# ScalarE fetches the last piece of every eighth group row by row, beside SyncE's three in eight

## What is computed

```python
h = relu(layernorm(x))
# first layer: relational convolution, 8 edge types
xW  = einsum('nd,rde->nre', h, W_rel)
agg = segment_sum(xW[src, edge_type], dst)
g   = gelu(layernorm(agg + h @ W_self + b_conv)); y = h + g
x   = x + y + (gelu(layernorm(y) @ W1 + b1) @ W2 + b2)
# second layer: attention with 4 heads of 32
h   = relu(layernorm(x)); xt = h @ W.T + bias
alpha = leaky_relu(alpha_src[src] + alpha_dst[dst])
x   = x + segment_sum(xt[src] * segment_softmax(alpha, dst), dst)
```

## Time and profile before

| | |
|---|---|
| time, median of 3 runs | 4385.58 us (4385.05 to 4386.91) |
| profiled execution, its own time | 4389.14 us |
| its span, first to last instruction | 4387.2 us |
| GpSimd busy | 3111.7 us, 71% of the span |
| VectorE, TensorE, ScalarE busy | 2539.8, 2471.2, 851.8 us |
| transfers of one row issued by SyncE | 4736 in each stage |

### The profile page before, as it was taken

One profiled execution on the slowest core, in us unless ns is written; L12 is line 12 of the kernel. 1 busy time (PEld: TensorE's weight loads), 2 busy tenths in 40 slices (PEclk: granted clock), 3 DMA queues, 4 the chain that ended last, 5 costly groups with the idle time before them and its releaser, 6 DMA issues.

```text
span 4387.2 us, 66590 instructions
## 1 busy us (share of the span) xinstructions
PE 2471.2 (56%) x13797; PEld 2079.8 (47%) x13902; DVE 2539.8 (58%) x7085; ACT 851.8 (19%) x2937; POOL 3111.7 (71%) x3284
## 2 busy tenths in 40 slices
PE   8833444444444444444444666666666666666665
PEld 3332443344334333334334555556566555565555
DVE  7742343343434434344345777777777777777777
ACT  5400110111101111011112222222222222222222
POOL 2177777777777777777737777777777777777774
PEclk9966676777777777777676777777777777777877
DMA  9622222222222222222214222222222222222221
GB/s 319 255 54 54 59 64 60 61 62 59 64 59 62 62 59 64 59 62 62 58 38 114 56 59 61 59 59 61 59 62 59 59 62 59 62 59 59 61 58 45
DMA packets 187072, 314.55 MB, mean 72 GB/s; under 512 B 67132, under 2 KB 117910, under 8 KB 185977
## 3 DMA queue, kind: packets, MB, share of 16 engines
q0 software_dynamic: 104128, 216.79, 21.2%
q1 hardware_dynamic: 38907, 68.15, 4.5%
q10 hardware_dynamic: 43634, 25.41, 2.0%
HBM read 238.50 MB, written 71.59 MB: 71 GB/s over the span
## 4 chain that ended last, share of the span: by engine, by line
POOL 37%; issue 28%; PE 21%; DVE 9%; DMA 2%; ACT 2%; DVEq 0%; POOLq 0%; ACTq 0%; SPq 0%
POOL G L612 37%; PE bank L1696 9%; PE quad L1741 3%; PE quad L1747 2%; DMA xt_table<-w_all 2%; DVE A L1226 1%; PE quad L1736 1%; PE quad L1638 1%; PE bank L1638 1%; PE bank L1639 1%; PE quad L1639 1%; ACT w_all L822 1%; PE quad L1783 1%; DVE stats L183 1%; PE bank L1769 1%
## 5 line engine op out<-in xcount | busy, mean ns | idle before, releaser
L612 POOL DMA_INDIRECT G<-rel_table,idx x1611 | 1532.1, 951 | 637.5 <-issue 491.4
L612 POOL DMA_INDIRECT G<-xt_table,idx x1627 | 1539.8, 946 | 557.5 <-issue 557.5
L1828 PEld LDWEIGHTS quad<-ident,top 128*128 128x128 f32 x3328 | 581.6, 275 | 227.9 <-issue 227.4
L1828 PE MATMUL quad<-ident,top 128*128 128x128 f32 x3328 | 595.3, 362 | 146.7 <-DVEq L1430 146.7
L1191 DVE SCALAR_TENSOR_TENSOR agg<-bank,sel,agg 128x128 f32 x208 | 63.5, 346 | 995.9 <-PE bank L1696 980.4
L1859 PE MATMUL bank<-M,onehot 128*128 128x132 f32 x3328 | 438.4, 287 | 156.6 <-DVE M L1479 152.2
L1859 PEld LDWEIGHTS bank<-M,onehot 128*128 128x128 f32 x3328 | 404.2, 196 | 188.4 <-issue 188.4
L1696 PE MATMUL bank<-G,onehot 128*128 128x128 f32 x1638 | 270.4, 342 | 362.0 <-issue 349.4
L1696 PEld LDWEIGHTS bank<-G,onehot 128*128 128x128 f32 x1638 | 266.6, 259 | 366.5 <-issue 366.5
L1844 PE MATMUL bank<-Z,w_all 128*128 128x8 f32 x832 | 159.4, 320 | 373.4 <-issue 363.8
L881 ACT ACTIVATE M<-G,M 128x32 f32<-128x32 f32 x1664 | 363.8, 308 | 13.6 <-ACT M L876 0.4
(11 more groups left out here) (324 smaller groups left out, 3618.9 us busy)
## 6 DMA issues: line engine op xcount, KB each, us to landing
side<-rel_table SPq DMA_DIRECT2D x4736, 0.5 KB
side<-xt_table SPq DMA_DIRECT2D x4736, 0.5 KB
rel_table<-G SPq DMA_DIRECT2D x98, 512.0 KB, 3.5
G<-rel_table,idx POOLq DMA_INDIRECT x1627, 2.5
G<-xt_table,idx POOLq DMA_INDIRECT x1627, 7.0
xt_table<-w_all ACTq DMA_DIRECT2D x23, 264.0 KB
x_mid<-X ACTq DMA_DIRECT2D x23, 256.0 KB
out<-A ACTq DMA_DIRECT2D x23, 256.0 KB
```

The source lines that it names most:

```text
L612: g.indirect_dma_start(out=G[:, s, c, 0:width], out_offset=None, in_=table, in_offset=bass.IndirectOffsetOnAxis(ap=idx[:, s, c:c + 1], axi ...
L1828: ins = t.matmul(banks[j][:, hd * P:(hd + 1) * P], top[:, j, hd:hd + 1].to_broadcast([P, P]), ident[:, :], start=False, stop=(hd == HEADS ...
```

## The change

Eleven more groups leave their last piece out of GpSimd's gathers: 16, 24, 32, ... 96. ScalarE fetches these rows, with the same one-row transfers, into a fourth side buffer, and by a third line of places. GpSimd so issues 15 gathers for these groups too, in both stages.

In the first stage (`first_rows`) the line is loaded behind the index copy of the third group ahead of the target, and 32 rows with two register loads of 16 stand behind each of the index copies of the groups target - 2 to target + 1. In the attention (`att_rows`) the line is loaded in the round of group target - 11, and 16 rows with one register load stand behind the index copy in each of the eight rounds target - 10 to target - 3. ScalarE then copies the buffer into `G` as for the others. SyncE's rows stay as they are, and only the values of its waits are counted anew.

```diff
+ACT_STEP = 8
+ACT_FIRST, ACT_LAST = 16, 96
+ACT_ROWS = 16
...
+def by_sync(g):
+    return g <= ROW_LAST and g % ROW_OF in ROW_AT
+def by_act(g):
+    return ACT_FIRST <= g <= ACT_LAST and g % ACT_STEP == 0
 def by_rows(g):
-    return g <= ROW_LAST and g % ROW_OF in ROW_AT
-ROWED = [g for g in range(GROUPS) if by_rows(g)]
+    return by_sync(g) or by_act(g)
+ROWED = [g for g in range(GROUPS) if by_sync(g)]
+ACTED = [g for g in range(GROUPS) if by_act(g)]
+MOVED = [g for g in range(GROUPS) if by_rows(g)]
...
-        line = sb("line", [1, 2, P], i32)
-        side = sb("side", [P, SIDES, XT])
+        line = sb("line", [1, 3, P], i32)
+        side = sb("side", [P, SIDES + 1, XT])
...
+            def act_line_load(k, gr):
+                act.dma_start(line[0:1, 2, :], row_places[gr:gr + 1, k, :]).then_inc(act_line, 16)
+            def act_rows(k, gr, lo, hi):
+                q = ACTED.index(gr)
+                if lo == 0:
+                    act.wait_ge(act_line, 16 * (k * len(ACTED) + q + 1))
+                    if k == 0 and q:
+                        act.wait_ge(agg_done, ACTED[q - 1] + 1)
+                    elif k and q:
+                        act.wait_ge(side_moved, MOVED.index(ACTED[q - 1]) + 1)
+                    elif k:
+                        act.wait_ge(agg_done, ACTED[-1] + 1)
+                    act_stop(act)
+                for p in range(lo, hi, ACT_ROWS):
+                    places = load_places(mybir.EngineType.Activation, k, line[0:1, 2, p:p + ACT_ROWS], ACT_ROWS)
+                    for j in range(ACT_ROWS):
+                        act.dma_start(row_into(k, SIDES, p + j), row_at(k, places[j])).then_inc(acted[k], 16)
+            def first_rows(gr):
+                for target in ACTED:
+                    if gr == target - 3:
+                        act_line_load(0, target)
+                    if 0 <= gr - (target - 2) < 4:
+                        act_rows(0, target, (gr - target + 2) * 32, (gr - target + 3) * 32)
+            def att_rows(gr):
+                for target in ACTED:
+                    if gr == target - 11:
+                        act_line_load(1, target)
+                    if 0 <= gr - (target - 10) < 8:
+                        act_rows(1, target, (gr - target + 10) * 16, (gr - target + 11) * 16)
...
                 if not last:
                     load_indices(n * SLOTS + (LAG + 1) * SLOTS)
+                    first_rows(n * SLOTS + (LAG + 1) * SLOTS)
...
                     next_indices(1, gr, (s + 1) % SLOTS, fetched(seat2, gr))
+                    att_rows(gr)
```

More of the change, by code:

```diff
@@ L445, in load_x, with rows_there, load_places, row_at @@
             eng.dma_start(x_res[:, lo:hi, :], x[lo * P:hi * P, :].rearrange("(b p) d -> p b d", p=P)).then_inc(s_x[lo // WIDE], 16)
+        def rows_there(k, gr):
+            if by_act(gr):
+                return SIDES, (acted[k], 16 * P * (ACTED.index(gr) + 1))
+            b, there = side_of(ROWED.index(gr))
+            return b, (rowed[k][b], there)
+        table_bytes = [rel_table.rearrange("a d -> (a d)").bitcast(u8), xt_table.rearrange("a d -> (a d)").bitcast(u8)]
+        row_bytes = (4 * D, 4 * XT)
+        def load_places(engine, k, at, count):
+            _, places = nc.values_load_multi_w_load_instructions(
+                at, engines=[engine], min_val=0, max_val=(BLOCKS * P * R * row_bytes[0], BLOCKS * P * row_bytes[1])[k] - row_bytes[k],
+                skip_runtime_bounds_check_because="a place is a node of the inputs times the bytes of a row")
+            assert len(places) == count
+            return places
+        def row_at(k, place):
+            return table_bytes[k][bass.ds(place, row_bytes[k])].rearrange("(o b) -> o b", o=1)
+        def row_into(k, b, p):
+            return side[p:p + 1, b, 0:row_bytes[k] // 4].bitcast(u8)
         block = ctx.enter_context(nc.Block())
@@ L498, in fetch_rows @@
                 for p in range(0, P, LOADED):
-                    _, at = nc.values_load_multi_w_load_instructions(
-                        line[0:1, m % 2, p:p + LOADED], engines=[mybir.EngineType.SP], min_val=0, max_val=(BLOCKS * P * R * row_bytes[0], BLOCKS * P * row_bytes[1])[k] - size,
-                        skip_runtime_bounds_check_because="a place is a node of the inputs times the bytes of a row")
+                    places = load_places(mybir.EngineType.SP, k, line[0:1, m % 2, p:p + LOADED], LOADED)
                     for j in range(LOADED):
-                        sp.dma_start(side[p + j:p + j + 1, b, 0:size // 4].bitcast(u8),
-                                     table_bytes[k][bass.ds(at[j], size)].rearrange("(o b) -> o b", o=1)).then_inc(rowed[k][b], 16)
+                        sp.dma_start(row_into(k, b, p + j), row_at(k, places[j])).then_inc(rowed[k][b], 16)
             load_line(0, 0)
@@ L547, in _ @@
                 if m >= SIDES:
-                    sp.wait_ge(side_moved, m - SIDES + 1)
+                    sp.wait_ge(side_moved, MOVED.index(ROWED[m - SIDES]) + 1)
                 else:
-                    sp.wait_ge(agg_done, ROWED[len(ROWED) - SIDES + m] + 1)
+                    sp.wait_ge(agg_done, ROWED[m - SIDES] + 1)
                 fetch_rows(1, m)
@@ L908, in move_side @@
                 if gr < MAIN and by_rows(gr):
-                    m = ROWED.index(gr)
-                    b, there = side_of(m)
-                    act.wait_ge(rowed[1][b], there)
+                    b, there = rows_there(1, gr)
+                    act.wait_ge(*there)
                     if gr >= SLOTS:
@@ L1551, in landed_in @@
                 there = [(gathered[1][gr % SLOTS], fetched(seat2, gr))]
-                return there + [(side_moved, ROWED.index(gr) + 1)] if by_rows(gr) else there
+                return there + [(side_moved, MOVED.index(gr) + 1)] if by_rows(gr) else there
             scores(groups, c, 0, 0, landed_in(0))
@@ L1688, in add_edges @@
                     if c == CHUNKS - 1 and beside is not None:
-                        b, there = side_of(beside)
+                        b, there = rows_there(0, beside)
                         rows_of = side[:, b, 0:D]
-                        pe.wait_ge(rowed[0][b], there)
+                        pe.wait_ge(*there)
                         pe_stop(pe)
@@ L1712, in add_group @@
                     landed = [(last_gathered[k], 16 * CHUNKS // PARTS) for k in range(PARTS)]
-                add_edges(g, seat(g), g % 2, landed, beside=ROWED.index(g) if by_rows(g) else None)
+                add_edges(g, seat(g), g % 2, landed, beside=g if by_rows(g) else None)
             for g in range(2):
```

9 lines of the change are left out of this document (6 added, 3 removed).

## The result

The changed kernel takes 4355.69 us (median of 4 runs, 4354.19 to 4357.44), the kernel before 4385.32 us on the same chip (4 runs, 4384.7 to 4386.91): ratio 0.9931, interval 0.9917 to 0.9945, so 29.6 us less. Forecast were 4358.1 us and 27.5 us less. The profiled execution took 4356.89 us with a span of 4354.9.

The account below looks back on a forecast made before the run. GpSimd's back-to-back gathers were taken to bound both stages. Two stages at 13.8 us less gave 27.5 us off the profiled 4389.1, so 4361.6; less 3.6 us for its lying above the median, 4358.1 us, range 4352 to 4374.

Parts of the forecast that it names:

- What bounds the kernel: Both stages: GpSimd's gathers stand back to back, one every 1.2515 us, and set how long each stage lasts.
- The 27.5 us: Whole kernel: eleven gathers fewer in each stage at 1.2515 us, 13.8 us a stage, 27.5 us less in all.
- ScalarE's prices: ScalarE's queue: 0.32 us a row, 1.17 us a load of 16 places, 12.6 us for 32 rows.
- The bound of 0.44: ScalarE's queue: the most one row could cost, 0.44 us, making 32 rows with two loads 16.4 us.
- First stage: Four places of 12.6 us of rows in two quads: delays made up there, nothing lost on the path.
- the third place: First stage, rows behind the copy at 1741.99: the self product's four normalizations start 10.2 us late.
- Attention: 6.3 us of rows in nearly every round, covered by 0.7 us and then 4 us more.
- VectorE could go 2 us a round faster: Attention: VectorE follows GpSimd, waiting 90 times for landings, 184.7 us in all, so has 2 us a round spare.
- SyncE: Its three sets take 153.6 us against GpSimd's 155.2; it keeps pace, with end leads of 62 and 20 us.
- rival 1: Both stages: SyncE's and ScalarE's issues hold each other up, 0.135 us a row; 190 us slower, 4575 us; chance 9%.
- rival 2: Part of the gain lost: ScalarE's row over 0.6 us or SyncE losing some 50 ns; 4368 to 4380 us; 6%.
- rival 3: Something else ends the stages at the same time, so the change makes no difference; 4385 us; chance 2%.

Follow-up runs that it names:

- experiment 2: Against the changed kernel: the last gathers of the eleven groups left out in both stages, nobody fetches those rows; 4355.5 us, ratio 0.9933.
- experiment 3: Changed kernel with ScalarE taking the last piece in one stage only: first stage alone 4368.15 us, attention alone 4371.49 us.
- experiment 8: The kernel before, unchanged, profiled a second time; one run, 4387.12 us.
- experiment 1: Against the changed kernel: ScalarE still issues its rows, but GpSimd keeps all gathers and nobody uses the rows; 4384.66 us, ratio 1.0.
- experiment 7: Changed kernel with the attention's 16 rows a round moved behind the eviction of the turned one-hots; 4357.56 us, ratio 0.9936.
- experiments 4 and 6: Variants of the changed kernel with other row loads ahead of the attention's eviction: 4 is e_two, 4516.15 us; 6 is e_burst, e_half and e_quarter.
- e_two: Changed kernel with 21 groups instead of eleven, a second side buffer and line, 32 rows ahead of the eviction in every attention round; 4516.15 us, ratio 1.0285.
- e_burst: Changed kernel with the attention's 128 rows of a group in one round instead of eight, ahead of the eviction; 4732.33 us, ratio 1.0785.
- e_half: Changed kernel with the attention's rows of a group as 32 in each of four rounds, ahead of the eviction; 4382.08 us, ratio 0.9992.
- e_quarter: Changed kernel with the attention's rows of a group as 64 in each of two rounds, ahead of the eviction; 4621.49 us, ratio 1.0539.
- experiment 6: Changed kernel with the attention's 128 rows a group spread over one, four or two rounds instead of eight; 4732.33, 4382.08 and 4621.49 us.

## Why the prediction was right

**What bounds the kernel.** Shown: GpSimd's gathers set both stages (the waits after, and experiment 2, where leaving 22 of them out gives 29.5 us by itself).

**The 27.5 us.** Right in mechanism, 2 us small: one term of the first stage was missing. Price and count hold in the attention (13.8 forecast, 13.5 and 12.8 measured in experiment 3 and between the traces). The first stage gave 16.8 and 17.8. The 3 to 4 us above 13.8 are no part of my account: I took all gathers to be alike, though in the earlier trace rows the longest of the first stage lasts 2321 ns and that of the attention 998. Fewer of the long ones, which all start beside VectorE's dense instructions, stand in the changed kernel, 11 for 23 in experiment 8 (experiment 3). That it came out that way round is luck, since nothing in the change aims at it. That the profiled execution lay 3.6 us above the median was taken off at the end; experiment 8 supports this: its attention gathers stand 1.9 ns closer. And the 1.2515 us should have been 1.2496: 0.04 us of the 27.5, nothing.

**ScalarE's prices.** 0.32 us forecast for a row, 0.325 measured by the median; 1.17 us for a load of 16, measured 1.20; 12.6 us for 32 rows, measured some 12.5. The bound of 0.44 was far off.

**First stage.** Right: the third place pushes the self product's normalizations, 11.7 us late against 10.2 forecast. The Gelu of the next quad starts 32.5 us behind the same store (1761.60 - 1729.14), before 23.6 us (1765.16 - 1741.57): 8.9 us late, forecast 8. VectorE reads its result at 1774.38, 12 us behind its end, forecast 11. TensorE's self transposes wait 172.2 us in all and VectorE 180.6 behind them. By experiment 1, whose first stage is as long as that of the kernel before, none of it reaches GpSimd.

**Attention.** The outcome was right, two of its numbers were not. I had the eviction end 0.7 us before TensorE wants it. The changed kernel's round:

```profile
3216.68 0.55 ACTq L818 DMA_DIRECT2D side<-xt_table  x1
3216.76 0.73 ACT L956 ACTIVATE M<-G,M 128x32 f32<-128x32 f32 x3
...
3217.39 0.31 ACT L956 ACTIVATE M<-G,M 128x32 f32<-128x32 f32 x1
...
3217.64 4.54 ACTq L818 DMA_DIRECT2D side<-xt_table  x14
...
3222.22 0.60 ACT L942 ACTIVATE w_all<-bank 128x512 f32<-128x512 bf16 x1 [4.43 <-issue]
...
3226.25 1.04 PE L1919 MATMUL bank<-Z,w_all 128*128 128x8 f32 x8 [4.20 <-DVEq L1522]
```

The first rows are issued at 3216.68, while the activations of L956 still run, the last of them to 3217.70: the queue had gone ahead of its engine, by 1.02 us. The eviction ends at 3222.82, 3.4 us before TensorE wants it, and TensorE waits for VectorE's sequencer. It isn't so in every round: in 13, one or two in eight, TensorE does wait for the eviction, up to 6.7 us and 54.6 in all. By experiment 7, which has no such rows ahead of it, this costs nothing that can be told. And "VectorE could go 2 us a round faster" was an average of its waits; its rounds without any wait are 18.2 us (145.3 / 8) against 19.4 for GpSimd's groups, so 1.2 us. That took nothing from this forecast, but my expectations in experiments 4 and 6 went wrong by it. For `e_two` and `e_burst` I gave VectorE 2 us a round to make up; it has 1.2, and 1.0 in `e_two`, where GpSimd's eight groups take 153.6. For `e_half` and `e_quarter` I took 17.5 us for every round without rows, which is the shortest and not the mean. The lateness itself was too small as well: 1 to 3 us forecast for 32 rows in `e_two` against 3.4, 16 against 17.2 for 64, 39 against 44.2 for 128.

**SyncE.** Right: three sets take 153.7 us. Its lead at the end of the attention is 4225.2 - 4208.3 = 16.9 us, forecast 20. Nothing waits for it; the copies into `G` wait 4 times and 11.5 us in all for side rows.

**The queues don't hold each other up.** Right, and experiment 1 shows it: 2816 more rows on ScalarE's queue, no time more. The rows of SyncE beside one of ScalarE start 1 ns later than the others, where rival 1 had 0.135 us, and the 2525 rows of SyncE that overlap one of ScalarE's in time last 230.3 ns for 230.0. Rival 1 is refuted, and so are rival 2 (its first condition, a row over 0.6 us, stands at 0.325) and rival 3.

## What to carry to other kernels

Here one queue's own pace set the time. Each gather taken from it gave its whole interval: eleven of 1.25 us gave 13.5 us in the attention. Another engine's idle queue could carry the work, two queues side by side, at no cost that the runs can tell: 4384.66 us with 2816 more rows and 4384.97 without. Where in that queue the work was put decided: the same 32 rows a round cost 130 us ahead of an activation that others wait for and saved 49 behind it. To know what a repeated lateness costs, compare the period with it against the period of the engine that sets the pace, and take the late engine's own period from rounds in which it waits for nothing. The excess of a period was paid in each: eleven times it was 44, 273 and 380 us in experiment 6, and the attention with its end grew by 34, 270 and 379. The lead only put off a part of it, 25, 18 and 15 us, most of which came back as a longer end.

## What the runs showed of the hardware that was not expected

- Rows of one piece issued on two queues at once did not slow SyncE's: 0.331 us between its rows beside one of ScalarE against 0.330 elsewhere, and 230.3 against 230.0 ns for one (changed kernel).
- ScalarE's queue issued transfers while activations ahead of them still ran: the first row at 3216.68, the end of the last activation of L956 at 3217.70 (changed kernel).
- The attention's gathers of one program started 1.2515 us apart in one execution (1.252 by the median) and 1.2496 in another; in the twelve profiles of these kernels other than the first the median was 1.249 each time.
- In the first stage 7 to 23 of some 1500 gathers lasted 1.14 to 1.63 us for 0.944. Each started while VectorE ran an instruction of the dense part and ended 0.81 to 0.82 us behind it, or behind the next where that followed at once (experiment 3).
